# A two-layer graph kernel on one core: outgoing table cleared from ScalarE's queue, two chunks' degrees on VectorE, the last weight turned in node tiles 4 to 8

## The chip, the cores and the metric

The kernel runs on one core of a Trainium2 chip. The metric is the time of one execution on the device in microseconds. TensorE is PE, VectorE DVE, ScalarE ACT, GpSimd POOL and SyncE SP in the rows. SP computes nothing here: it issues loads and stores, one after the other, each behind its waits.

## What is computed

```python
def sage(h, W_self, W_neigh, b):            # deg_inv = 1 / max(in-degree, 1)
    agg = segment_sum(h[src], dst)
    return h @ W_self + (agg * deg_inv[:, None]) @ W_neigh + b

h   = relu(sage(x, W_self0, W_neigh0, b0))
x   = layernorm(x + sage(h, W_self1, W_neigh1, b1))
# GCN layer on x, with self loops, deg = out-degree + 1
y   = x @ W.T + b
msg = deg[row]**-0.5 * deg[col]**-0.5 * y[col]
out = layernorm(x + segment_sum(msg, row))
```

x is 1250 x 1024 in fp32, there are 20000 edges sorted by dst, and all five weights are 1024 x 1024.

## The kernel before

**Data.** The 1250 nodes are 10 tiles of 128 rows (the last has 98), the 1024 features 8 blocks (KD = 8). The graph becomes two dense tables of 1280 x 1280 counts in DRAM, `adj_in` and `adj_out`, 6.55 MB each. They are set to zero, then GpSimd scatters into them, 160 indirect DMAs of 125 numbers for each table. A table is read back in panels of 1280 x 256 (1280 KB). Every fp32 product is split: an operand is kept as a rounded high part (written by ScalarE) and the rest as low part (written by VectorE), and three matmuls stand for one.

**Stages on PE.** All have one order, written out by hand in program text.

- *Node tiles 0 to 9* (`linear(N0, t)`, L1429): x W_neigh0. A tile is 24 steps of two 512-wide matmuls; after step 4 the next x tile is transposed (`turn_tile`, L1370). ScalarE runs per tile `turn_hi(t + 1)`, `evict_hi(N0, t)` and `store_turned(t + 1)`, and VectorE the low parts. In the last tile ScalarE also splits the rows of W_self0 (`split_hi(S0, k)`), rows 0 to 3 ahead of `evict_hi(N0, 9)`.
- *self_turned* (L1484): x W_self0, turned, in 24 steps of 24 matmuls, chunks of 4, 4 and 2 node tiles. At the last step of a chunk its eight blocks are finished one by one; ScalarE evicts each into one of four `staged` slots and stores it to `s0t_scr` (`store_s0`). Block i waits for the store of block i - 4, and PE waits for the evicted bank before it opens the same bank in the next chunk.
- *mean0*: the neighbour sum, in four chunks of 2, 4, 2, 2 node tiles (`CHUNKS`), eight feature blocks each, so 32 cells m = 0 to 31, a cell being 20 matmuls (L1515) against the chunk's panels. At the head of a chunk PE makes the degrees: ten matmuls of ones against the panels (L1504). VectorE turns them into 1/deg (L1183, L1185), and then per cell scales the bank (L1191, frees it: `h_free`) and adds the self block that SP fetched from `s0t_scr` (L914, `h_sum`). After blocks 1 and 2 of a chunk it reduces panels for the out-degree (`dpart`, L1197). After block 2 PE turns 1/deg to columns by tiny matmuls (L1522), which VectorE copies to `dinv` after block 5.
- *products* (L1572): the two products of layer 1 by a seven-product scheme; *mean1* (L1589): neighbour sum and first layernorm, node tile by node tile, where after each of tiles 1 to 8 PE transposes one row block of the GCN weight (`turn_weights`, L1380), ScalarE copies it out (L857) and stores it to `wt_scr`; *gather* (L1606) and the last linear (L1429, L1413).

**SP in mean0.** The self fetches are issued in order of m. Four slots serve cells 0 to 15, so fetch m waits for `h_sum` m - 3 (from m = 4 on). Behind fetch 15 stand the panels of chunk 2, behind fetch 23 those of chunk 3; both also wait for their part of the scatters (`load_chunk_1`):

```python
            for m, (c, d) in enumerate(H_BLOCKS):                     # L509
                if m >= 4:
                    sp.wait_ge(h_sum, fetch_free(m))                  # m - 3 for m < 16
                sp.dma_start(fetch_slot(m)..., s0t_scr[...])          # L514
                if m in (15, 23):
                    load_chunk_1(2 + m // 17)                         # L425
```

**The outgoing table.** GpSimd clears `adj_out` with four DMAs in the middle of its first group of scatters (L636), writes the ones of its diagonal at group 5 (L655), and scatters into it after `adj_in`. The zeros lie where node tile 6 will be evicted, so `evict_hi(N0, 6)` waits for both clears.

## Time and profile before

| | us |
|---|---|
| median of 3 runs | 851.29 |
| lowest, highest | 848.52, 852.38 |
| the profiled execution, its own time | 849.59 |
| its span | 847.9 |

The profile has a page (busy time of each engine, the span in 40 slices, DMA queues, the chain of work that ended last, the costliest groups) and views that the trace answers: timelines of one engine, waits, and DMA issues in a window. A timeline row gives the start, the length, the line, the tile written and the ones read, and in brackets how long the engine stood idle before it and what released it. PE's rows are modelled, and a row reaches a little into the next, so the distance between starts is the better length.

### The profile page before, as it was taken

The page shows a single profiled execution, that of the slowest core. Times are in us where ns is not written, and L with a number is a line of the kernel's source. Part 1 is how long each engine was busy: PE and PEld are TensorE (multiplying, and loading weights), DVE is VectorE, ACT ScalarE, POOL GpSimd, SP SyncE. Part 2 cuts the span into 40 slices and gives each one's busy share as a digit, 9 for nine tenths or more (in the row PEclk, how much of TensorE's full clock was granted, in tenths as well). Part 3 has the DMA queues.
Part 4 walks back from the last instruction along what each step waited for, and adds up shares of the span by engine and source line. Part 5 has one row for each costly group of instructions (what it writes and reads, how often), then busy time and mean ns, then how long its engine had stood idle before and what let it go on. Part 6 is the DMA issues. An engine that isn't in the chain of part 4 may idle for free.

```text
span 847.9 us, 11000 instructions
## 1 busy us (share of the span) xinstructions
PE 830.6 (98%) x4295; PEld 707.9 (83%) x4295; DVE 461.3 (54%) x714; ACT 177.4 (21%) x218; POOL 459.1 (54%) x343
## 2 busy tenths in 40 slices
PE   8999999999999999999999999999999999999996
PEld 6888888888897899788888888778889889988885
DVE  6465568200017565897544677775556435455555
ACT  4111132110111113353123112222222122200000
POOL 5028887787777887885888788788620000000000
PEclk9999999999999999999999999999999999999999
DMA  9977965463776425668876668267877649555551
GB/s 332 380 304 267 350 193 168 125 176 75 213 236 180 122 57 133 249 237 286 298 282 222 243 220 284 62 176 214 240 245 255 223 150 295 189 199 199 198 193 46
DMA packets 99480, 180.52 MB, mean 213 GB/s; under 512 B 15474, under 2 KB 75898, under 8 KB 94048
## 3 DMA queue, kind: packets, MB, share of 16 engines
q1 hardware_dynamic: 60144, 124.17, 44.0%
q10 hardware_dynamic: 26896, 40.65, 13.3%
q0 software_dynamic: 12384, 14.95, 7.6%
q8 instruction: 36, 0.59, 0.3%
q14 instruction: 20, 0.16, 0.1%
HBM read 107.08 MB, written 72.43 MB: 212 GB/s over the span
## 4 chain that ended last, share of the span: by engine, by line
PE 61%; POOL 15%; DMA 9%; issue 8%; DVE 5%; SPq 1%; ACT 1%; POOLq 0%; ACTq 0%; DVEq 0%
PE ps L1572 19%; POOL adj_in L643 14%; PE ps L1429 12%; PE ps L1606 10%; PE ps L1589 9%; PE ps L1515 8%; DMA adj_in<-u 4%; DMA first_rows<-in_L_gnn_W_neigh 1%; DMA spare<-in_x 1%; DMA xin<-s0t_scr 1%; PE ps L1413 1%; DVE u L914 1%; PE ps L1380 1%; SPq L514 1%; DVE sacc L1303 0%
## 5 line engine op out<-in xcount | busy, mean ns | idle before, releaser
L643 POOL DMA_INDIRECT adj_out<-loops,idx_out x160 | 245.2, 1533 | 65.4 <-issue 65.4
L643 POOL DMA_INDIRECT adj_in<-mult,idx_in x160 | 198.1, 1238 | 86.8 <-issue 86.8
L1572 PE MATMUL ps<-u 128*128 128x512 f32 x840 | 190.7, 389 | 1.4 <-DVE u L914 1.4
L1572 PEld LDWEIGHTS ps<-u 128*128 128x128 f32 x840 | 157.6, 188 | 34.2 <-issue 1.6
L1484 PE MATMUL ps<-wx 128*128 128x512 f32 (+1 forms) x576 | 109.4, 351 | 1.3 <-ACT outb L761 1.3
L1484 PEld LDWEIGHTS ps<-wx 128*128 128x128 f32 x576 | 93.9, 189 | 16.9 <-ACT outb L761 1.9
L1429 PE MATMUL ps<-u 128*128 128x512 f32 x432 | 98.2, 389 | 0.0
L1515 PE MATMUL ps<-wx,u 128*128 128x256 f32 (+5 forms) x640 | 94.8, 309 | 1.2 <-DVE ht L1191 1.2
L1589 PE MATMUL ps<-u,panel_tiles 128*128 128x512 f32 (+1 forms) x400 | 93.9, 393 | 1.9 <-DVE u L914 1.9
L1429 PEld LDWEIGHTS ps<-u 128*128 128x128 f32 x432 | 81.0, 188 | 16.8
L1515 PEld LDWEIGHTS ps<-wx,u 128*128 128x128 f32 (+1 forms) x640 | 86.6, 191 | 8.2 <-DVE ht L1191 1.6
L1429 PE MATMUL ps<-wx 128*128 128x512 f32 x384 | 89.6, 392 | 0.0
L1589 PEld LDWEIGHTS ps<-u,panel_tiles 128*128 128x128 f32 (+1 forms) x400 | 74.5, 188 | 18.1 <-issue 2.3
L1429 PEld LDWEIGHTS ps<-wx 128*128 128x128 f32 x384 | 71.4, 188 | 14.6
L1606 PE MATMUL ps<-u,wx 128*128 128x512 f32 (+2 forms) x480 | 74.5, 317 | 0.0
L1606 PEld LDWEIGHTS ps<-u,wx 128*128 128x128 f32 x480 | 67.2, 191 | 6.6
L1183 DVE TENSOR_SCALAR dinv_row<-ps 128x256 f32<-128x256 f32 (+2 forms) x4 | 1.9, 480 | 84.7 <-PE ps L1504 84.7
L844 ACT ACTIVATE std<-mv,eps 128x1 f32<-128x1 f32 x20 | 5.9, 295 | 163.8 <-DVE mv L1028 163.8
L761 ACT ACTIVATE outb<-ps,b0c 128x512 f32<-128x512 f32 (+1 forms) x24 | 14.8, 618 | 94.1 <-PE ps L1484 87.2
L1347 DVE SCALAR_TENSOR_TENSOR outb<-ps,dscale,xin 128x1024 f32<-128x1024 f32 x9 | 11.6, 1283 | 40.8 <-PE ps L1429 40.8
L816 ACT ACTIVATE ht<-ht 128x256 f32<-128x256 f32 (+2 forms) x32 | 14.9, 466 | 83.1 <-DVE ht L914 83.1
L1006 DVE TENSOR_TENSOR u<-ps,u 128x1024 fp32r<-128x1024 f32 x10 | 12.2, 1224 | 33.3 <-ACT u L721 33.2
(167 smaller groups left out, 779.8 us busy)
## 6 DMA issues: line engine op xcount, KB each, us to landing
left_scr<-u SPq DMA_DIRECT2D x7, 2560.0 KB, 9.5
u<-left_scr SPq DMA_DIRECT2D x7, 2560.0 KB, 9.6
xt_scr<-wx ACTq DMA_DIRECT2D x10, 1024.0 KB, 9.9
u<-xt_scr SPq DMA_DIRECT2D x10, 1024.0 KB, 5.1
wx<-xt_scr SPq DMA_DIRECT2D x16, 512.0 KB, 4.0
adj_in<-u POOLq DMA_DIRECT2D x4, 1600.0 KB, 25.3
adj_out<-u POOLq DMA_DIRECT2D x4, 1600.0 KB, 16.1
wx<-adj_in SPq DMA_DIRECT2D x5, 1280.0 KB, 7.1
```

The source lines that it names most:

```text
L514: sp.dma_start(fetch_slot(m)[:, 0:CHUNKS[c][1] * T], s0t_scr[d, :, lines(CHUNKS[c])]).then_inc(s0_in[m % 8], 16)
L643: pool.indirect_dma_start(table, bass.IndirectOffsetOnAxis(ap=index[0:EP, j:j + 1], axis=0), counts[0:EP, j:j + 1], None, bounds_check=CEL ...
L761: nc.scalar.activation(staged[i % 4][:, 0:width], ps[:, d, 0:width], ACT.Identity, bias=b0c[:, d:d + 1]).then_inc(s0_free, 1)
L816: nc.scalar.activation(cell, cell, ACT.Relu).then_inc(h_done, 1)
L1006: nc.vector.tensor_tensor(u[:, :, t, 1, :], pair_bank(acc_pair(q, t)).rearrange("p (a j) -> p a j", a=2), u[:, :, t, 0, :].bitcast(F32), A ...
L1347: nc.vector.scalar_tensor_tensor(z, pair_bank(acc_pair(GCN, t))[:, :], dscale[:, t:t + 1], rest, ALU.mult, ALU.add).then_inc(acc_free, 1)
L1429: ins = nc.tensor.matmul(acc[:, cols], left_tile[:, t % 2, k, left * T:(left + 1) * T], w_row(q, k, right)[:, cols], start=(i == 0), stop= ...
L1484: ins = nc.tensor.matmul(block_of[d], w[:, k, left, d * P:(d + 1) * P], where[right], start=(first and left + right == 0), stop=(final and ...
L1515: ins = nc.tensor.matmul(ps[:, h_bank(m), 0:width].rearrange("p (n j) -> p n j", n=n // 2), typed(u0_part(k, h, d), exact), typed(panels[0 ...
L1572: ins = nc.tensor.matmul(ps[:, product_bank(g, i, p), :], left_op[n % 2][:, p, k, left, :], right_op[n % 2][:, k, right, :], start=(not on ...
L1589: ins = nc.tensor.matmul(pair_bank(acc_pair("MEAN1", t))[:, cols], typed(p1_tile[t][0:rows(k), k, :], exact), typed(u[0:rows(k), n, k, h, ...
L1606: ins = nc.tensor.matmul(ps[:, g_bank(KD * c + d), 0:width].rearrange("p (n j) -> p n j", n=n // 2), typed(yd[:, h, d * P:(d + 1) * P], ex ...
```

## The change

Five things are moved.

1. `adj_out` is cleared by five DMAs from ScalarE's queue in self_turned, after steps 2 to 6, from zeros that VectorE writes into `xin`. The diagonal follows from ScalarE before s0 block 8. GpSimd's clears and diagonal go, as does the wait of `evict_hi` for `cleared_out`. Since `xin` is the source, SP waits for the clears before it fetches self blocks, and it now fetches 0 to 3 at step 20 of self_turned.
2. The degrees of chunks 0 and 1: VectorE sums the panels over their ten row tiles (L1213 in the new file) into `sacc`, rounds them into `colsum`, and PE does one matmul of ones against it (`degrees`), after block 3 of the chunk.
3. The degrees of chunks 2 and 3 stay ten matmuls. The tiny turns of 1/deg go in all chunks: SP stores each row to `dinv_scr` and loads all as columns after mean0.
4. The turns of the GCN weight go from mean1 to node tiles 4 to 8, by `WEIGHT_ROWS`: row blocks 0; 1, 2; 3, 4; 5, 6; 7. They stand after steps 10 and 18 of the tile. SP loads them into `raw`, and the loads of the first rows of W_self0, which use `raw` and `outb`, wait for them.
5. `bias` and `colsum` share memory, so the load of b1 goes behind the degrees.

```diff
+    WEIGHT_ROWS = {4: (0,), 5: (1, 2), 6: (3, 4), 7: (5, 6), 8: (7,)}
...
             for t in range(2, NT):
                 load_x(t)
+                for k in WEIGHT_ROWS.get(t - 1, ()):
+                    sp.wait_ge(w_lo_done, KD * S0)
+                    if k >= 2:
+                        sp.wait_ge(wt_turned, k - 1)
+                    sp.dma_start(raw[:, k % 2, :], w_gcn[k * P:(k + 1) * P, :]).then_inc(wt_in[k % 2], 16)
             for k in range(4):
-                sp.wait_ge(w_lo_done, KD * S0)
+                if k < 2:
+                    sp.wait_ge(wt_turned, 7 + k)
+                else:
+                    sp.wait_ge(wt_stored[k % 2], 16 * KD // 2)
                 load_w(S0, k)
...
+                if i == 20:
+                    sp.wait_ge(adj_out_set, 16 * CLEARS)
+                    for m in range(4):
+                        fetch_self(m)
...
                 if m in (15, 23):
                     load_chunk_1(2 + m // 17)
+                if d == 6:
+                    t0, n = CHUNKS[c]
+                    sp.wait_ge(dinv_row_done, c + 1)
+                    sp.dma_start(dinv_scr[lines(CHUNKS[c])].rearrange("(a j) -> a j", a=1), dinv_row[0:1, c % 2, 0:n * T]
+                                 ).then_inc(dinv_stored[c % 2], 16)
...
+            def keep_turned(k):
+                act.wait_ge(wt_turned, k + 1)
+                if k >= 2:
+                    act.wait_ge(wt_stored[k % 2], 16 * (k // 2))
+                else:
+                    act.wait_ge(w_lo_done, KD * S0)
+                nc.scalar.activation(outb[:, k % 2, :], pair_bank(3), ACT.Copy).then_inc(wt_copied, 1)
...
                     turn_hi(t + 1)
+                    for k in WEIGHT_ROWS.get(t, ()):
+                        keep_turned(k)
                     evict_hi(N0, t)
...
+            for a in range(CLEARS):
+                act.wait_ge(*s0_used_by(a + 2))
+                act.dma_start(runs[a, :, :, :], zeros_out.unsqueeze(1).broadcast_to([P, ZERO_TIMES, ZERO_PART])).then_inc(adj_out_set, 16)
...
                 if d == 0:
+                    if c < 2:
+                        dve.wait_ge(m1_full[c], 16 * n // 2)
+                        nc.vector.tensor_reduce(sacc[:, 0:width].rearrange("p (n j) -> p n j", n=n // 2),
+                                                m1_panels[c][:, :, :, :].bitcast(F32).rearrange("p k n j -> p n j k"), AX_X, ALU.add
+                                                ).then_inc(colsum_done, 1)
+                        dve.wait_ge(colsum_done, 2 * c + 1)
+                        nc.vector.tensor_copy(colsum[:, 0:width], sacc[:, 0:width]).then_inc(colsum_done, 1)
                     dve.wait_ge(deg_full, c + 1)
...
-                        if d == 2:
-                            pe.wait_ge(dinv_row_done, c + 1)
-                            for i in range(n):
-                                ins = nc.tensor.matmul(ps[:, 6 + c % 2, i:i + 1], dinv_row[0:1, c % 2, i * T:(i + 1) * T],
-                                                       ones_nt[0:1, 0:1], start=True, stop=True)
-                            ins.then_inc(dcol_full, 1)
+                        if (c, d) in ((0, 3), (1, 3)):
+                            degrees(c, width, exact)
```

The order of instructions at three places. First PE in mean0, chunks 0 to 2. `ones_r` is the operand of ones; the rows of before:

```order
L1504 MATMUL ps<-wx,ones_r 128x256 x10
L1515 MATMUL ps<-wx,u 128x256 x60
L1522 MATMUL ps<-ones_nt,dinv_row 128x1 x2
L1515 MATMUL ps<-wx,u 128x256 x100
L1504 MATMUL ps<-wx,ones_r 128x512 x10
L1515 MATMUL ps<-wx,u 128x512 x60
L1522 MATMUL ps<-ones_nt,dinv_row 128x1 x4
L1515 MATMUL ps<-wx,u 128x512 x100
L1504 MATMUL ps<-wx,ones_r 128x256 x10
```

and of the change:

```order
L1563 MATMUL ps<-wx,u 128x256 x80
L1540 MATMUL ps<-colsum,ones_r 128x256
L1563 MATMUL ps<-wx,u 128x256 x80
L1563 MATMUL ps<-wx,u 128x512 x80
L1540 MATMUL ps<-colsum,ones_r 128x512
L1563 MATMUL ps<-wx,u 128x512 x80
L1551 MATMUL ps<-wx,ones_r 128x256 x10
```

The degrees of chunk 1 stood ahead of its first cell and now stand behind its fourth (80 matmuls are four cells).

Second VectorE, from the last cell of chunk 0 to the first two of chunk 1, before:

```order
L1191 TENSOR_TENSOR ht<-ps,dinv_row 128x256
L914 SCALAR_TENSOR_TENSOR ht<-ht,xin 128x256
L1183 TENSOR_SCALAR dinv_row<-ps 128x512
L1185 RECIPROCAL dinv_row<-dinv_row 128x512
L1191 TENSOR_TENSOR ht<-ps,dinv_row 128x512
```

and in the change:

```order
L1229 TENSOR_TENSOR ht<-ps,dinv_row 128x256
L943 SCALAR_TENSOR_TENSOR ht<-ht,xin 128x256
L1213 TENSOR_REDUCE sacc<-wx 128x512
L1217 CAST colsum<-sacc 128x512
L1221 TENSOR_SCALAR dinv_row<-ps 128x512
L1223 RECIPROCAL dinv_row<-dinv_row 128x512
L1229 TENSOR_TENSOR ht<-ps,dinv_row 128x512
```

The reduction and the rounding stand ahead of the row work, which waits for the one matmul, and with it everything behind.

Third PE in node tile 5 of the change, between the turns of x tiles 6 and 7 (L1406; `raw` holds the weight rows); before, 48 matmuls stood there in one piece:

```order
L1406 MATMUL ps<-ident,xin 128x128 x8
L1468 MATMUL ps<-wx 128x512 x12
L1417 MATMUL ps<-ident,raw 128x128 x8
L1468 MATMUL ps<-wx 128x512 x16
L1417 MATMUL ps<-ident,raw 128x128 x8
L1468 MATMUL ps<-wx 128x512 x20
L1406 MATMUL ps<-ident,xin 128x128 x8
```

Two blocks of eight transposes came in; the eight blocks of this kind between the tiles of mean1 went out.

## Rows read from the trace of the kernel before

**Rows 1.** Page: busy us, share, instructions; then the granted TensorE clock by slice (9: 90% or more).

```profile
PE 830.6 (98%) x4295; PEld 707.9 (83%) x4295; DVE 461.3 (54%) x714; ACT 177.4 (21%) x218; POOL 459.1 (54%) x343
...
PEclk9999999999999999999999999999999999999999
```

**Rows 2.** Waits of PE: line, releaser, us in total, times, longest.

```profile
PE ps L1589 <- DVE u L914: 1.9, 1, 1.9
...
PE ps L1380 <- ACT late L857: 1.1, 1, 1.1
```

**Rows 3.** PE's timeline, mean0: start us, us, line, shapes, count, [idle before <-releaser].

```profile
237.41 1.37 PE L1504 MATMUL ps<-wx,ones_r 128*128 128x256 f32 x10
238.62 7.36 PE L1515 MATMUL ps<-wx,u 128*128 128x256 f32 x60
245.91 0.60 PE L1522 MATMUL ps<-ones_nt,dinv_row 1*128 1x1 f32 x4
246.44 12.26 PE L1515 MATMUL ps<-wx,u 128*128 128x256 f32 x100
258.54 2.46 PE L1504 MATMUL ps<-wx,ones_r 128*128 128x512 f32 x10
262.19 14.04 PE L1515 MATMUL ps<-wx,u 128*128 128x512 f32 x60 [1.20 <-DVE ht L1191]
276.16 1.05 PE L1522 MATMUL ps<-ones_nt,dinv_row 1*128 1x1 f32 x8
277.14 23.22 PE L1515 MATMUL ps<-wx,u 128*128 128x512 f32 x100
300.19 1.35 PE L1504 MATMUL ps<-wx,ones_r 128*128 128x256 f32 x10
```

**Rows 4.** VectorE's timeline, mean0: second self add, then chunk 1's row work, cells, reduction.

```profile
258.32 0.43 DVE L914 SCALAR_TENSOR_TENSOR ht<-ht,xin 128x256 f32<-128x256 f32 x1 [4.12 <-DMA xin<-s0t_scr]
...
267.10 0.68 DVE L1183 TENSOR_SCALAR dinv_row<-ps 128x512 f32<-128x512 f32 x1
...
271.21 0.69 DVE L1191 TENSOR_TENSOR ht<-ps,dinv_row 128x512 f32<-128x512 f32 x1
...
273.87 2.81 DVE L1197 TENSOR_REDUCE dpart<-wx 128x10 f32<-128x2560 f32 x1
```

**Rows 5.** SP's queue, mean0: issue of fetches 5 to 15, then of chunk 2's panels.

```profile
258.83 25.08 SPq L514 DMA_DIRECT2D xin<-s0t_scr  x11
287.54 0.37 SPq L425 DMA_DIRECT2D wx<-adj_in  x1
```

**Rows 6.** DMA issues (at 224, 240 and 69 us; then of the whole run): KB each, median us to landing.

```profile
wx<-adj_in SPq DMA_DIRECT2D x1, 1280.0 KB, 6.4
...
wx<-adj_in SPq DMA_DIRECT2D x1, 1280.0 KB, 12.8
...
xt_scr<-wx ACTq DMA_DIRECT2D x1, 1024.0 KB, 4.2
...
wt_scr<-late ACTq DMA_DIRECT2D x8, 512.0 KB, 5.0
...
raw<-in_L_gnn_W_self SPq DMA_DIRECT2D x4, 512.0 KB, 10.5
```

**Rows 7.** PE's timeline: a turn block in node tile 8, one in mean1.

```profile
105.99 1.04 PE L1370 MATMUL ps<-ident,xin 128*128 128x128 f32 x8
106.79 1.40 PE L1429 MATMUL ps<-wx 128*128 128x512 f32 x5
...
575.06 1.04 PE L1380 MATMUL ps<-ident,late 128*128 128x128 f32 x8
```

**Rows 8.** ScalarE's timeline, self_turned: evictions 0 and 4 of the s0 blocks.

```profile
165.87 0.69 ACT L761 ACTIVATE outb<-ps,b0c 128x512 f32<-128x512 f32 x1 [32.51 <-PE ps L1484]
...
170.30 0.69 ACT L761 ACTIVATE outb<-ps,b0c 128x512 f32<-128x512 f32 x1 [0.46 <-PE ps L1484]
```

**Rows 9.** PE's timeline, start of the kernel.

```profile
1.47 4.21 PE L1634 MATMUL ps<-ones_r 128*128 128x512 f32 x9 [1.47 <-DVE scrap_dve L1043]
```

137 lines of the change are left out of this document (71 added, 66 removed).

## The prediction, made before the changed kernel ran

> **What bounds the kernel now.** The page's engine row comes first: PE is busy 830.6 us of a span of 847.9 us and its granted clock reads 9 in every slice [rows 1]. So PE never rests: 17.3 us of idle is all that removed waits can give, the rest must come out of PE's own list. The list of PE's waits says which part of that idle this change can reach: 1.1 us at L1380, released by ScalarE's copy of a turned weight [rows 2], and 1.20 us in mean0 at L1515, released by VectorE [rows 3]. The chain of waits is less use: a third of it is GpSimd's scatters and the loads behind them, but PE was working through nearly all of that time. So I read PE's own timeline through mean0 [rows 3], then the engines that feed PE there.
>
> **1. Degrees of chunks 0 and 1, and the turning of 1/deg.** PE drops ten 256-wide column sums (237.41 to 238.62, 1.21 us) and ten 512-wide ones (ten at 4.61/20 = 0.23 us, 2.30 us, from the cell duration below) and gets one matmul of each width, 0.12 and 0.23 us. It also drops the small turns L1522: 245.91 to 246.44 is 0.53 us for two node tiles (records 245.91 x4), 276.16 to 277.14 is 0.98 us for four, and chunks 2 and 3 have two node tiles each. Sum: (1.21 - 0.12) + (2.30 - 0.23) + 3 x 0.53 + 0.98 = 1.09 + 2.07 + 2.57 = 5.73 us off PE [rows 3]. The 1.20 us wait of 262.19 goes too: VectorE was late there since its second self block landed only at 258.3 [rows 4], behind the panels of chunk 1 on SP's queue. The change fetches blocks 0 to 3 in self_turned. Together 6.93 us.
>
> What VectorE gets: a reduction of 2560 numbers, then one of 5120. The nearest row is the contiguous reduction of 2560, 2.81 us [rows 4]; the new ones read with a stride, which no row shows. I take 2.8 and 5.5 us, and twice that as the bad bound. The first lies in front of mean0, where VectorE has nothing to do. The second starts after cell 7, about 24 us into mean0, and must be done at 38 us, when PE has finished cell 11: covered by 8 us, and by 2.5 us at the bad bound.
>
> **2. What is late next: chunk 2's panels.** This is the part that decides. The degree matmul of chunk 1 now stands behind cell 11 (four cells into the chunk) and not ahead of cell 8. VectorE can't scale any cell of the chunk before it, so four cells pile up. From the start of the chunk's row work (267.10) to the first cell's scaling (271.21) is 4.11 us; two cells take 273.87 - 271.21 = 2.66 us, so 1.33 each; a dpart reduction takes 2.81 us and its short sum about 0.2 more [rows 4]. To the end of cell 11: 4.11 + 4 x 1.33 + 2 x 3.0 = 15.4 us, 15.6 with the last write. And SP's queue has h_sum 12 in it: fetch_self(15) waits for cell 11, since slot 15 mod 4 is the slot of 11, and the panels of chunk 2 are issued behind it (m in (15, 23)). Before, SP issued fetch 15 as the last of eleven, ending at 283.91, then stood until GpSimd's 144th scatter had landed and issued the panels at 287.54, still 12.6 us before PE wanted them at 300.19 [rows 3, 5].
>
> Count from mean0's start. Chunk 0: eight cells of 12.10/5 = 2.42 us (246.44 to 258.54) and one short matmul, 19.5 us. Cells 8 to 11: 4 x 4.61 (23.05/5, from 277.14 to 300.19) = 18.5 us, so the degree matmul goes at 38.0 and ends at about 38.4. Cell 11 is added at 38.4 + 15.6 = 54.0. SP issues fetch 15 and then the panels, at 54.5. A load of that size from this table took 6.4 us to landing when alone, 12.8 us behind its twin [rows 6]; with the small fetch 15 ahead I take 6.8, so 61.3. PE is through cell 15 at 19.5 + 36.9 + 0.23 = 56.7. It waits 61.3 - 56.7 = **4.6 us**, where it waited for nothing; the landing alone spreads this from 4.2 to 10.6. Net of mean0: -6.93 + 4.6 = -2.3 us. Nothing else there is late: cell 14 wants cell 8's bank back, free at 38.4 + 4.8 = 43.2 against 47.4; chunk 1's panels are issued earlier against PE than before, because GpSimd's list is shorter and PE comes later; stored 1/deg rows come back on SP long before mean1.
>
> **3. The weight turns.** Eight blocks of eight transposes leave mean1 and enter node tiles 4 to 8. A block is 1.04 us long in a node tile and in mean1, and the matmuls after it start 0.8 us behind its start [rows 7], so 6.4 us are moved and none saved; what goes is the 1.1 us wait at L1380 [rows 2]. ScalarE's eight copies, 1.4 us each at most by the 0.69 us of half the width [rows 8], go to an engine that is 21% busy [rows 1] and are waited for only by the next block, 16 matmuls later. Loads: each of rows 2 to 7 is issued when the row two before it is turned, a node tile (48 matmuls of 0.23 us, 11 us) or more ahead of use; a 512 KB load must stay under that. The tightest link is at the end: the store of row 7, then self weight row 3 into the same outb slot, then ScalarE's evict_hi(9), in order behind that split. The turn of x tile 9 stands at 105.99 [rows 7], and seven blocks by then shift it to 111.6; 0.8 us and twelve matmuls of 0.23 later row 7 is turned, done by 116.0; copied by 117.0; a store of a turned row took 5.0 us and a load of such a weight row 10.5 in traffic [rows 6], and no more than the store's 5 on a quiet queue, so row 3 lands between 127 and 132.5. PE leaves tile 9 at 111.6 + 0.8 + (28 + 12 + 48 matmuls) x 0.23 + 0.8 = 133.4, and only then has ScalarE anything to evict. Covered by 1 to 6 us, and PE wants that bank 18 matmuls later still. Cost taken: 0, bounds 0 and 3.
>
> **4. The outgoing table.** GpSimd loses four clears and two diagonal stores from its queue and is done with its scatters a little earlier. Nothing of it shows in PE's time: chunk 2's panels now wait for VectorE, and chunk 3's had landed in time before, with PE now later. The clears go to ScalarE's queue, the fifth at the end of self_turned's step 6, about 1 us before the stores of the finished s0 blocks. Those stores share its queue, and the eviction of block 4 waits for store 0. Before, eviction 0 started at 165.87 and eviction 4 at 170.30, so each took 1.11 us and the eighth was done at about 174.4 [rows 8]. PE had finished block 0 at 165.6 and wanted the eighth bank 42 matmuls later (21 of the rest of step 7, 21 of step 8), at 175.2: 0.8 us to spare. The fifth clear is issued at 164.9 in those times. A 1024 KB store landed in 4.2 us [rows 6], so 1280 KB take 5 to 7 us beside the loads of that stage, store 0 lands at 171 to 173, and eviction 4 starts 0.6 to 2.7 us late. Cost 0 to 1.9 us; I take **0.5**.
>
> The row shows no store queued behind a clear. The Trainium skill (DMA: Bandwidth & Descriptors, section "Queues, rings and completion order") says that one issuing engine's DMAs use the same rings and are consumed in ring order; by that the store waits for the clear as I assumed. If DMAs of one queue overtook each other, this cost would be 0.
>
> **Sum.** -6.93 + 4.6 - 1.1 + 0.5 = -2.9 us. Against the profiled execution of 849.6 us (span 847.9) that is 846.7 us, -0.34%; the median of the runs shown is 851.29 us, 1.7 us higher, so 848.4 us.
>
> **The rivals.**
> A. *Chunk 2's panels are not late.* If SP didn't have to wait for cell 11, or VectorE caught up faster, the 4.6 us fall away: 848.4 - 4.6 = 843.8 us. For it: the wait depends on a slot number and on rows that I had to move. Against: every link is in program order, and the 15.6 us are measured. A shorter stall of 2 to 3 us, which is in reach of my errors, gives 846 to 847.
> B. *PE's clock falls in the new gap.* All slices of before stand at 2.4 GHz [rows 1], and the longest idle among them is 1.9 us [rows 2]. At the start of the kernel nine matmuls took 4.21 us, 0.47 each against 0.23 [rows 9], so PE ran for that stretch at half rate. If a 4.6 us gap brings that back, the same stretch costs 4.21 - 9 x 0.23 = 2.1 us more: 848.4 + 2.1 = 850.5 us, no change. The Trainium skill (TensorE: Matmul & The Clock Gate, section "HAM oscillation") says that a PE that waits for a transfer long enough is put back to half rate and starts slow again; this is that rule's time here, and no gap of before is long enough to show it.
> C. *The panel transfer lands late.* It costs 12.8 us, as for the twin at 240, and not 6.8: PE waits 10.6 us, the sum is +3.1, and with the clock fallen (+2.1) it is +5.2 us: 856.5 us, slower. It decides above 9.7 us of landing. For it: the same table's load did take that long when two were issued together. Against: here one is issued alone, and SP's next transfers stand behind it.
>
> **Numbers.** The forecast with its errors (846.5 to 850) gets 0.52; A 0.20; B 0.15; C and a late weight row in part 3 0.13. A measurement of this kernel can tell about 0.5%, or 4.3 us, from no change; the forecast of -2.9 us lies within that, but near its edge, so a share of it counts as faster. Faster by over 0.5%: 0.20 from A and 0.12 from the forecast's edge, 0.32. Slower by over 0.5%: 0.10. Within: 0.58. The range reaches from A, 843.5, to past B, 852.5.
>
> **What would show it.** PE's timeline in mean0: about 19.5 us for chunk 0, then a gap of 4.6 us ahead of the ten column sums of chunk 2, released by a DMA into wx from adj_in; no gap ahead of cell 8. SP's timeline: the panels of chunk 2 issued 54 us after mean0's start. VectorE: a reduction of about 5.5 us behind cell 7. ScalarE: the eviction of s0 block 4 starts 1 to 3 us later than its cadence. PE's waits: L1380's is gone, no new one in node tiles 4 to 8, nor at self_turned's first blocks. The granted clock: full in the slice after the gap; below it for B. I am wrong if the gap is absent, if it is longer than 6 us, or if a wait for a weight row shows up in the first 130 us.

## The result, and the profile after

The changed kernel takes 852.25 us (median of 16 runs, 850.04 to 857.51), the kernel before in the same session 849.93 us (16 runs, 847.78 to 852.38): ratio 1.0032, 95% interval 1.0021 to 1.0043. So it is slower by 0.3%, where 848.4 us was forecast, that is 2.9 us off the 851.29 us of the three runs of before known then; off the 849.93 us measured beside the changed kernel it would have been 847.0. The profiled execution took 850.04 us (span 848.3). It is the fastest of the 16, and its mean granted clock is 0.996, while most of the others lie between 0.989 and 0.994.

Of both kernels the execution with the trace is compared below; for the kernel before that is a typical one (849.59 us), for the changed kernel its fastest.

The page's engine row, as [rows 1]: PE has 3.3 us less to do, and the span is 0.4 us longer.

```profile
PE 827.3 (98%) x4257; PEld 703.5 (83%) x4257; DVE 476.0 (56%) x715; ACT 178.6 (21%) x218; POOL 456.7 (54%) x337
```

PE's waits, as [rows 2]. L1380's wait is gone. New are the wait at L1551 (the column sums of chunk 2), 1.87 us of the 3.0 at L1523 (self_turned; the rest stood in before too) and a small one at the gather (L1648).

```profile
PE ps L1551 <- DMA wx<-adj_in: 5.0, 1, 5.0
PE ps L1523 <- ACT outb L797: 3.0, 6, 1.0
PE ps L1616 <- DVE u L943: 1.6, 1, 1.6
...
PE ps L1648 <- DMA panel_tiles<-adj_out: 0.5, 1, 0.5
```

PE's timeline through mean0, as [rows 3] (L1563 the cells, L1540 the one matmul of degrees, L1551 the ten of chunks 2 and 3):

```profile
247.74 9.76 PE L1563 MATMUL ps<-wx,u 128*128 128x256 f32 x80
257.33 0.28 PE L1540 MATMUL ps<-colsum,ones_r 128*128 128x256 f32 x1
257.45 28.12 PE L1563 MATMUL ps<-wx,u 128*128 128x256 f32 x160
285.41 0.39 PE L1540 MATMUL ps<-colsum,ones_r 128*128 128x512 f32 x1
285.64 18.53 PE L1563 MATMUL ps<-wx,u 128*128 128x512 f32 x80
309.12 2.49 PE L1551 MATMUL ps<-wx,ones_r 128*128 128x256 f32 x10 [4.95 <-DMA wx<-adj_in]
311.40 19.88 PE L1563 MATMUL ps<-wx,u 128*128 128x256 f32 x160
331.12 1.28 PE L1551 MATMUL ps<-wx,ones_r 128*128 128x226 f32 x10
```

No gap stands ahead of cell 8. The gap ahead of chunk 2 is there. Behind it the ten sums take 311.40 - 309.12 = 2.28 us, where ten such sums took 1.21 us before [rows 3]. The granted clock by windows tells why (columns: window, its length with the busy us of PE, PEld, DVE, ACT, POOL, then PEclk, DMA share, GB/s):

```profile
305.00:309.00 4.00, 0.00 (x0) 0.00 (x0) 3.95 (x4) 0.63 (x1) 3.41 (x2) 1.00 1.08 335
309.00:313.00 4.00, 3.88 (x19) 3.88 (x20) 1.32 (x2) 0.63 (x1) 3.38 (x3) 0.57 0.63 143
313.00:317.00 4.00, 4.00 (x36) 4.00 (x35) 1.79 (x4) 0.42 (x1) 3.09 (x4) 1.00 0.17 34
```

SP's queue, as [rows 5], and VectorE's second reduction, as [rows 4]:

```profile
266.49 30.99 SPq L476 DMA_DIRECT2D xin<-s0t_scr  x8
...
302.05 0.37 SPq L432 DMA_DIRECT2D wx<-adj_in  x1
...
319.55 0.37 SPq L432 DMA_DIRECT2D wx<-adj_in  x1
```

```profile
270.65 9.46 DVE L1213 TENSOR_REDUCE sacc<-wx 128x512 f32<-128x5120 f32 x1
280.14 0.43 DVE L1217 CAST colsum<-sacc 128x512 fp32r<-128x512 f32 x1
```

The reduction took 9.46 us, the first one 4.80 (from 241.58), where I had 5.5 and 2.8 and twice that as the bad bound. It ended 4.8 us before the matmul at 285.41.

In self_turned PE waits four times for ScalarE's evictions when it opens the banks again, 1.87 us together. The three matmuls behind each of the first three waits take 0.96 us, 0.32 each and not 0.23, so the stage loses more than the waits say:

```profile
181.26 0.96 PE L1523 MATMUL ps<-wx 128*128 128x512 f32 x3 [0.96 <-ACT outb L797]
182.76 0.96 PE L1523 MATMUL ps<-wx 128*128 128x512 f32 x3 [0.54 <-ACT outb L797]
183.91 0.96 PE L1523 MATMUL ps<-wx 128*128 128x512 f32 x3 [0.18 <-ACT outb L797]
185.05 2.33 PE L1523 MATMUL ps<-wx 128*128 128x512 f32 x9 [0.19 <-ACT outb L797]
```

The chain of waits (start, length, what) has changed its last part. In the changed kernel it runs through GpSimd up to the gather:

```profile
626.50 2.57 DMA adj_out<-loops,idx_out
629.09 6.54 DMA panel_tiles<-adj_out
635.68 13.48 PE ps L1648 x110
```

GpSimd's last scatter starts at 626.50 us. Before it started at 620.33. That bears on every mending below, and [rows 1 to 9] don't have it:

```profile
620.33 1.27 POOL L643 DMA_INDIRECT adj_out<-loops,idx_out  x1 [0.30 <-issue]
```

Set side by side, the starts of PE's stages say where the time went (us; the shift is the changed kernel's start less before's):

| PE starts | before | changed | shift | shift that the prediction's terms give |
|---|---|---|---|---|
| self_turned | 126.86 | 133.90 | 7.0 | 6.4 |
| mean0 | 237.41 | 247.74 | 10.3 | 6.9 |
| products | 342.64 | 351.82 | 9.2 | 4.6 |
| mean1 | 535.24 | 543.06 | 7.8 | 4.6 |
| gather | 635.34 | 635.68 | 0.3 | -2.9 |

The biggest step that wasn't forecast is self_turned. It takes 113.8 us and took 110.6, so 3.3 us more, where the term was 0.5. On the page its matmuls, 576 in both kernels, are busy 1.4 us longer and waited 1.7 us longer for ScalarE:

```profile
L1484 PE MATMUL ps<-wx 128*128 128x512 f32 (+1 forms) x576 | 109.4, 351 | 1.3 <-ACT outb L761 1.3
L1523 PE MATMUL ps<-wx 128*128 128x512 f32 (+1 forms) x576 | 110.8, 352 | 3.2 <-ACT outb L797 3.0
```

The rows of the later stages, before and changed:

```profile
342.64 190.66 PE L1572 MATMUL ps<-u 128*128 128x512 f32 x840 [1.43 <-DVE u L914]
535.24 18.57 PE L1589 MATMUL ps<-u,panel_tiles 128*128 128x512 f32 x80 [1.94 <-DVE u L914]
351.82 190.68 PE L1616 MATMUL ps<-u 128*128 128x512 f32 x840 [1.56 <-DVE u L943]
543.06 92.10 PE L1633 MATMUL ps<-u,panel_tiles 128*128 128x512 f32 x400 [0.56 <-DVE u L943]
```

### The profile page after: what moved, and what is told of

Read it like the earlier page. It is cut to its first block, busy times and chain, and to the rows that moved or that the text cites. A ratio compares the mean times of both kernels' runs of the same rounds, so it can differ in the third digit from the quotient of the medians.

```text
span 848.3 us, 10948 instructions
## 1 busy us (share of the span) xinstructions
PE 827.3 (98%) x4257; PEld 703.5 (83%) x4257; DVE 476.0 (56%) x715; ACT 178.6 (21%) x218; POOL 456.7 (54%) x337
## 2 busy tenths in 40 slices
DMA packets 102815, 180.52 MB, mean 213 GB/s; under 512 B 18038, under 2 KB 78465, under 8 KB 97896
## 4 chain that ended last, share of the span: by engine, by line
POOL 47%; PE 23%; issue 19%; DMA 7%; DVE 1%; POOLq 1%; SPq 0%; ACT 0%; DVEq 0%
POOL adj_out L663 26%; POOL adj_in L663 21%; PE ps L1468 12%; PE ps L1648 10%; DMA adj_in<-u 4%; DMA first_rows<-in_L_gnn_W_neigh 1%; PE ps L1450 1%; POOLq L663 1%; DMA panel_tiles<-adj_out 1%; DVE sacc L1339 0%; SPq L426 0%; DMA adj_out<-loops,idx_out 0%; PE ps L1669 0%; POOL adj_in L660 0%; DVE outb L1355 0%
## 5 line engine op out<-in xcount | busy, mean ns | idle before, releaser
L1523 PE MATMUL ps<-wx 128*128 128x512 f32 (+1 forms) x576 | 110.8, 352 | 3.2 <-ACT outb L797 3.0
L1523 PEld LDWEIGHTS ps<-wx 128*128 128x128 f32 x576 | 93.7, 189 | 20.4 <-ACT outb L797 5.4
L1563 PE MATMUL ps<-wx,u 128*128 128x256 f32 (+5 forms) x640 | 94.3, 309 | 0.0
L1633 PE MATMUL ps<-u,panel_tiles 128*128 128x512 f32 (+1 forms) x400 | 92.1, 392 | 0.6 <-DVE u L943 0.6
L1563 PEld LDWEIGHTS ps<-wx,u 128*128 128x128 f32 (+1 forms) x640 | 87.1, 192 | 6.6
L1468 PE MATMUL ps<-wx 128*128 128x512 f32 x384 | 91.9, 394 | 0.0
L1648 PE MATMUL ps<-u,wx 128*128 128x512 f32 (+2 forms) x480 | 74.5, 317 | 0.0
L1648 PEld LDWEIGHTS ps<-u,wx 128*128 128x128 f32 x480 | 67.2, 191 | 6.6
L1213 DVE TENSOR_REDUCE sacc<-wx 128x256 f32<-128x2560 f32 (+1 forms) x2 | 14.3, 7129 | 79.3 <-DMA wx<-adj_in 79.3
```

The lines of the kernel that those rows point to most:

```text
L1213: nc.vector.tensor_reduce(sacc[:, 0:width].rearrange("p (n j) -> p n j", n=n // 2), m1_panels[c][:, :, :, :].bitcast(F32).rearrange("p k n ...
L1468: ins = nc.tensor.matmul(acc[:, cols], left_tile[:, t % 2, k, left * T:(left + 1) * T], w_row(q, k, right)[:, cols], start=(i == 0), stop= ...
L1523: ins = nc.tensor.matmul(block_of[d], w[:, k, left, d * P:(d + 1) * P], where[right], start=(first and left + right == 0), stop=(final and ...
L1563: ins = nc.tensor.matmul(ps[:, h_bank(m), 0:width].rearrange("p (n j) -> p n j", n=n // 2), typed(u0_part(k, h, d), exact), typed(panels[0 ...
L1633: ins = nc.tensor.matmul(pair_bank(acc_pair("MEAN1", t))[:, cols], typed(p1_tile[t][0:rows(k), k, :], exact), typed(u[0:rows(k), n, k, h, ...
L1648: ins = nc.tensor.matmul(ps[:, g_bank(KD * c + d), 0:width].rearrange("p (n j) -> p n j", n=n // 2), typed(yd[:, h, d * P:(d + 1) * P], ex ...
```

## The theories

- **W, the waits.** The change loses its savings in the three new waits: chunk 2's panels, the evictions, and the clock behind them. Mended one by one, they give 3 to 7 us back.
- **H, GpSimd.** GpSimd's scatters bind as closely as PE's list did. Whatever PE saves ahead of a table is waited off when it wants the table. (For the gather alone the expectations call it G; other letters in them are explained where they stand.)
- **K, the clock.** A gap in PE's work costs more than its length, since the clock is lower behind it.

Three sessions of runs (e1 to e4, e9 to e12, e13 to e16) were made on chips where the kernel before takes 849.8 to 850.3 us. One, with e5 to e8, was made on a chip where it takes 871.0 us. So ratios to the kernel before of the same session are compared.

## Experiments on single parts

**e1, chunk 2's panels early.** Changed kernel with

```diff
-                if m in (15, 23):
+                if m in (13, 23):
                     load_chunk_1(2 + m // 17)
```

> The change, with chunk 2's panels issued behind self fetch 13 and not behind fetch 15, so that SP no longer waits for cell 11 before it issues them. Theory G (GpSimd's last scatter into the outgoing table, 6 us later than before the change, holds the start of the gather, so what PE saves ahead of it is lost): the 5.0 us wait and the slow start behind it go from mean0, a wait of 4 to 7 us appears ahead of the gather's first matmul, released by the load of the outgoing panels, and the time stays within 1.5 us of the change's 852.3. Theory P (PE's list and its own waits add up to the time, as I predicted): 5.0 us of wait and 1.4 us of half rate go, 846 us.

Measured: 852.44 us, ratio 1.0022 [1.0000, 1.0044]. The gap ahead of chunk 2 is gone, and the time is not. PE's waits:

```profile
PE ps L1648 <- DMA panel_tiles<-adj_out: 4.9, 1, 4.9
PE ps L1523 <- ACT outb L797: 2.1, 3, 1.1
PE ps L1616 <- DVE u L943: 1.9, 1, 1.9
PE ps L1551 <- DMA wx<-adj_in: 1.4, 1, 1.4
```

The wait of 5 us moved 330 us down the program, to the gather, released by the load behind GpSimd's last scatter. Another 1.4 us stands at chunk 3's column sums, and the granted clock is at 0.50 from 634 to 640 us, behind the wait at the gather.

**e2, e3, e4, the last 16 scatters into adj_out left out**, in the changed kernel, in e1 and in before:

```diff
-                for j in range(EC):
+                for j in range(EC - 16):
                     put(adj_out, idx_out, loops, j, scattered_out)
...
-            sp.wait_ge(scattered_out, 16 * EC)
+            sp.wait_ge(scattered_out, 16 * (EC - 16))
```

> The change, with the last 16 of the 160 scatters into the outgoing table left out, so GpSimd is done some 24 us earlier (those edges are missing from the second layer's sum). Theory G: the wait ahead of the gather, 0.5 us in the profiled execution and more in the typical one, goes; 849.5 to 851.5 us. Theory P: no change beyond 0.5 us, 851.8 to 852.5 us. Rival T (the clock after the 5 us gap varies between executions): no change either, with the same spread.

> The change, with chunk 2's panels behind fetch 13 and with the last 16 scatters into the outgoing table left out (those edges are missing from the second layer's sum). Theory G: only both together give the whole, 5.0 + 1.4 us of mean0 and the wait ahead of the gather: 843 to 846 us, at least 5 us under each of the two alone. Theory P: the same as the panels alone, 846 us.

> The kernel before, with the last 16 scatters into the outgoing table left out (those edges are missing from the second layer's sum). Theories G and P both: before the change the last scatter had landed 1 us before SP was free to load the panels, so nothing moves, ratio 0.999 to 1.001. If the ratio is under 0.998, the outgoing table held the kernel before too in its typical execution.

Measured: e2 855.71 us, ratio 1.0064 [1.0043, 1.0086]; e3 848.35, 0.9989 [0.9968, 1.0011], above the 843 to 846 us that I expected; e4 849.56, 0.9991 [0.9975, 1.0006]. No gather wait is left in e2 and e3. Against e1, e3 gives back 4.1 us, about what the gather had waited. Before gains nothing: its gather isn't held by GpSimd. e2 is a miss. It has six runs, and a mean clock of 0.992 like the changed kernel's. Its waits are the changed kernel's without the gather, with 3.1 us ahead of the products and not 1.6. Why it is 3 us slower is not explained. Its trace shows something else. Up to the last 16 scatters e2 is the changed kernel, and yet its 160th scatter starts at 307.27 us, where the changed kernel's starts at 316.49 and before's at 309.77. So when GpSimd comes to a table differs by 9 us between two executions of the same instructions, and e2 is slow with an early GpSimd: GpSimd can't be the whole cause of the changed kernel's time.

**e5, the turns back in mean1.** Changed kernel without part 3:

```diff
-                    if q == N0 and i in (10, 18) and i // 18 < len(WEIGHT_ROWS.get(t, ())):
-                        turn_weights(WEIGHT_ROWS[t][i // 18])
...
+                        if 1 <= t <= KD:
+                            turn_weights(t - 1)
```

(and the loads, copies and stores with them).

> The change without its third part: the weight is turned in mean1 again, its loads and stores with it; degrees and the clears from ScalarE's queue stay. Theory G (every wait of PE costs its length and, when it is 2 us or more, a stretch at half rate; the last scatter holds the gather since the rows' traffic in node tiles 4 to 8 slows GpSimd there): no wait ahead of the gather, last scatter at 617 to 621 us and not 626.5; the waits at the evictions (1.9 us) and for chunk 2's panels (5.0 and 1.4 us of half rate) stay; 850.5 to 852.5 us. Theory W (the turns in the node tiles themselves cost the time): 849 us or less. If GpSimd's last scatter stays at 626, the clears are what slows it.

**e6, the clears back on GpSimd.** Changed kernel without part 4:

```diff
-                act.wait_ge(*s0_used_by(a + 2))
-                act.dma_start(runs[a, :, :, :], zeros_out.unsqueeze(1).broadcast_to([P, ZERO_TIMES, ZERO_PART])).then_inc(adj_out_set, 16)
...
+                        if (g, c) == (0, RUN // 2) and not general_form:
+                            clear(adj_out, cleared_out)
```

> The change without its fourth part: GpSimd clears the outgoing table and writes its diagonal again; degrees and early turns stay. Theory G: no wait at the evictions of self_turned beyond the 1.3 us of before, full rate there; GpSimd's list is 4 us longer, so its last scatter starts at 628 to 631 us and the wait ahead of the gather grows from 0.5 to 4 to 7 us; 850 to 853 us. Theory P (waits add up, no GpSimd bound): 849 us.

**e7, part 1 alone**, the degrees in the kernel before (with the early self fetches):

```diff
+                    if c < 2:
+                        dve.wait_ge(m1_full[c], 16 * n // 2)
+                        nc.vector.tensor_reduce(sacc[:, 0:width]...)
...
+                        if (c, d) in ((0, 3), (1, 3)):
+                            degrees(c, width, exact)
```

> The change's first part alone (degrees of two chunks on VectorE, 1/deg by way of memory): turns in mean1 and clears on GpSimd as before. By my sum: 6.9 us off, 5.0 us of wait for chunk 2's panels and 1.4 us of half rate behind it on, so 849.3 us, ratio 0.998 to 1.001. It measures whether this part is worth anything as it stands.

**e8, three things mended**: e5 with e1's edit and the clears a step earlier:

```diff
             for a in range(CLEARS):
-                act.wait_ge(*s0_used_by(a + 2))
+                act.wait_ge(*s0_used_by(a + 1))
```

> Turns in mean1 as before, degrees as changed with chunk 2's panels issued behind self fetch 13, clears from ScalarE's queue one step earlier each (after steps 1 to 5). Theory G: no wait at chunk 2, the evictions' waits back at 1.3 us, GpSimd early, so the full 6.9 us of mean0: 842 to 845 us, ratio 0.991 to 0.994. Theory P gives the same here. If the evictions still wait, the five clears disturb them by their load and not by the place of the last one.

Measured on the chip where before takes 871.03 us:

| | us | ratio | 95% |
|---|---|---|---|
| e5, turns back | 874.82 | 1.0050 | 1.0026 to 1.0073 |
| e6, clears back | 883.12 | 1.0160 | 1.0135 to 1.0185 |
| e7, part 1 alone | 869.70 | 0.9993 | 0.9972 to 1.0013 |
| e8, three mended | 863.52 | 0.9923 | 0.9901 to 0.9945 |

Part 1 alone takes 5.7 us of work off PE and gains nothing that can be measured: its panels of chunk 2 come 4.7 us late too. In e6 PE waits 10.6 us in the node tiles for a copy of a turned weight row, which stands on ScalarE behind `evict_hi(N0, 6)` and its wait for GpSimd's clears. So part 4 is what makes part 3 possible. Three expectations were missed here: e5's last scatter starts at 626.13 us and not at 617 to 621, e6 doesn't wait at the gather, and e6 is far above its 850 to 853 us even as a ratio. By e5's own words the clears would then be what slows GpSimd, but e8 has them on ScalarE's queue too, and its last scatter starts at 617.64. e8 looked like the answer, 0.8% faster than before.

## The same edits on a chip like the first

**e9**: changed kernel with e1's and e8's edits, turns in the node tiles. **e10**: with the clears' edit alone. **e11**: e5 with e1's edit. **e12**: e8 once more.

> The change with two edits: chunk 2's panels issued behind self fetch 13 (before fetches 14 and 15), and each of the five clears of adj_out one step earlier in self_turned. The turns of the weight stay in node tiles 4 to 8; that alone sets it apart from the kernel with three edits, which measured 0.9923 of before. Theory G (with the panels early, GpSimd's last scatter holds the gather, and the moved turns are what PE no longer has in mean1 to cover it): a wait at the gather, released by the DMA panel_tiles<-adj_out, of 4 to 6 us, no wait of over 1 us at the column sums, the eviction waits in self_turned under 1 us; ratio to before 0.995 to 1.000, so some 3 to 5 us above the kernel with the turns in mean1. Rival (where the turns stand makes no difference, and the kernel with three edits is fast because of the clears alone): no wait or a small one at the gather, ratio 0.990 to 0.994.

> The change with one edit: each of the five clears one step earlier in self_turned, so that the fifth is issued a whole step (24 matmuls) before the first s0 store and not about 1 us before it. If the fifth clear holds store 0 and so eviction 4, the four waits that summed to 1.87 us around 181 to 185 fall to under 0.4 us, the slice 180 to 200 us stays at the full granted clock, and the ratio is 0.996 to 1.001 (the change: 1.0032). The waits at chunk 2's column sums (about 5 us) and at the gather (about 0.5, up to 3 since PE comes earlier) stay. Rival (the evictions are late from a DMA load of that stage, whatever stands before them on ScalarE's queue): the same waits, ratio 1.002 to 1.004.

> The change with the turns of the weight in mean1 as before and chunk 2's panels behind self fetch 13; the clears stay where the change has them. It differs from the kernel with three edits (0.9923 of before) by the step of the clears alone. If the clears' place is worth the eviction waits and a stretch at the lower clock, 2 to 4 us: ratio 0.995 to 0.998, waits at self_turned's evictions 2 to 4 us. If the clears' place is worth little and the panels and the turns made it: 0.991 to 0.993. No wait at chunk 2's column sums over 1.5 us and none at the gather.

> The kernel with three edits once more (turns in mean1 as before, panels behind fetch 13, clears a step earlier), on this chip and beside the other three. It measured 0.9923 [0.9901, 0.9945] on a chip where both kernels were 2.5% slower. If it is worth its 6 to 7 us wherever it runs: 0.990 to 0.995. If that was the other chip, on which PE's clock fell more often: 0.996 to 0.999, which is what the sum of its parts gives from the profile alone (5.73 + 1.2 of part 1, less some of the new waits).

Measured (before 850.27 us, 27 runs):

| | turns | panels | clears | us | ratio | 95% |
|---|---|---|---|---|---|---|
| e9 | node tiles | early | early | 849.60 | 1.0005 | 0.9983 to 1.0026 |
| e10 | node tiles | as changed | early | 851.90 | 1.0021 | 1.0001 to 1.0041 |
| e11 | mean1 | early | as changed | 852.82 | 1.0037 | 1.0025 to 1.0049 |
| e12 | mean1 | early | early | 853.44 | 1.0047 | 1.0028 to 1.0066 |

e12 is e8, and it is slower than before here. e9, e11 and e12 came out above every ratio that I had written down for them or for the theory behind them, e9 without the wait at the gather that I expected (0.4 us), and e10 in the rival's range although its waits fell as in the first theory. W is not enough, then, and the trace of the mended kernel had to say more. PE's timeline and SP's queue of e12 in mean0 (L1554 the column sums of chunks 2 and 3):

```profile
298.62 2.26 PE L1554 MATMUL ps<-wx,ones_r 128*128 128x256 f32 x10 [1.87 <-DMA wx<-adj_in]
324.31 2.48 PE L1554 MATMUL ps<-wx,ones_r 128*128 128x226 f32 x10 [3.54 <-DMA wx<-adj_in]
```

```profile
317.88 0.37 SPq L432 DMA_DIRECT2D wx<-adj_in  x1
```

and GpSimd's last scatter into adj_in, the 160th:

```profile
314.50 1.19 POOL L664 DMA_INDIRECT adj_in<-mult,idx_in  x1 [0.30 <-issue]
```

PE waits for chunk 3's panels, which SP issues when that scatter has landed. The load lands 6.4 us later, at 324.3, and neither SP's queue nor VectorE has a part in it. The same three rows of the kernel before read: scatter 160 at 309.77, panels issued at 314.12 and 7.1 us to landing, so 321.2; and PE begins these sums at 321.30 without idle time:

```profile
309.77 1.19 POOL L643 DMA_INDIRECT adj_in<-mult,idx_in  x1 [0.30 <-issue]
```

```profile
314.12 0.37 SPq L425 DMA_DIRECT2D wx<-adj_in  x1
```

```profile
wx<-adj_in SPq DMA_DIRECT2D x1, 1280.0 KB, 7.1
```

```profile
321.30 1.32 PE L1504 MATMUL ps<-wx,ones_r 128*128 128x226 f32 x10
```

So before had 0.1 us to spare at this place, and its list of waits shows nothing there. With GpSimd as it ran in that execution and PE's order otherwise unchanged, no microsecond saved ahead of chunk 3 could have been kept. Behind both waits of e12 the clock is at half as well (0.50 from 300 to 302 and from 324 to 328 us).

On the slower chip PE needs longer up to chunk 3 and GpSimd doesn't: scatter 160 starts at 314.28 us in e8 and at 314.50 in e12, and PE makes the degrees of chunk 1 at 286.91 and at 277.99. PE reached chunk 3's sums at 326.17 us in e8, 2.9 us after its panels were due (issued 316.92, plus 6.4), and waited for nothing. That fits a gain there and a loss here. It isn't shown, since no run on the slower chip shortens GpSimd's list and before has no trace there.

## GpSimd's list shortened, and one gap by itself

**e13, e14, e15**: in e12, e9 and before the last 8 of 160 scatters into adj_in are left out, so that all that GpSimd does behind them comes about 12 us earlier (8 times 1.5).

```diff
-                        put(adj_in, idx_in, mult, g * RUN + c, scattered_in[sum(g >= need for need in NEEDS)])
+                        if (g, c) < (GROUPS - 1, RUN - 8):
+                            put(adj_in, idx_in, mult, g * RUN + c, scattered_in[sum(g >= need for need in NEEDS)])
```

(and SP's wait for the last part of the scatters lower by 8.)

> The kernel with three edits (turns in mean1 as before, panels behind fetch 13, clears a step earlier; 1.0047 of before) with the last 8 of 160 scatters into adj_in left out, so that its table lacks 1000 of 20000 edges; everything on GpSimd behind them, the whole of adj_out too, comes 12 us earlier (8 times 1.5). Theory H (GpSimd's scatters and the load behind them set the start of chunk 3 at 321 to 325 us whatever PE does, and later the gather, so that what PE saves before is waited off): the 3.5 us wait at chunk 3's column sums goes, the gather waits for nothing, and the ratio falls from 1.0047 to 0.994 to 0.999. Rival (the savings are lost to the lower clock and to ScalarE's and VectorE's waits, and the wait at chunk 3 would come out elsewhere): ratio 1.001 to 1.005.

> The kernel with two edits (turns in node tiles 4 to 8, panels behind fetch 13, clears a step earlier; 1.0005 of before) with the last 8 of 160 scatters into adj_in left out. Theory H: here the turns stand ahead of mean0 and fill the time that would be waited off, so chunk 3 hardly waited, but the gather is near its bound; PE's list is then the bound in both kernels and this one comes out near the one with the turns in mean1: 0.993 to 0.998, a gain of 0.3 to 0.6%. Rival: no gain, 0.999 to 1.002.

> Control: the kernel before with the last 8 of 160 scatters into adj_in left out. Its chunk 3 started exactly when its panels had landed (321.2 against 321.30) and without idle time, so PE's list was just the bound and nothing is gained: 0.998 to 1.001 by either theory. A ratio under 0.997 would say that before waited for GpSimd in many of its executions, though not in the profiled one.

**e16**, one gap in the kernel before:

```diff
-                if m in (15, 23):
-                    load_chunk_1(2 + m // 17)
+                if m in (20, 23):
+                    load_chunk_1(2 + m // 23)
```

> The kernel before with one edit: chunk 2's panels are issued behind self fetch 20 and not 15. Fetch 20 waits for cell 14, which is added at about 298 us, so the panels land at about 304.5 and PE waits some 4 us ahead of chunk 2's column sums, which stand at 300.19. Nothing else changes. If a wait costs its own length alone: +4 us, ratio 1.004 to 1.006. If the clock falls behind it as in the changed kernel (ten sums in 2.28 us and not 1.21) and PE goes slower for that stretch only: +5 to +6 us, 1.006 to 1.008. If chunk 3's start is pinned by its panels at 321 us plus, and the gap pushes everything: the same, since chunk 3's panels then have landed in time.

Measured (before 849.94 us, 17 runs):

| | us | ratio | 95% | same kernel with all scatters |
|---|---|---|---|---|
| e13, turns in mean1 | 846.53 | 0.9953 | 0.9938 to 0.9968 | 1.0047 (e12) |
| e14, turns in node tiles | 841.48 | 0.9898 | 0.9885 to 0.9911 | 1.0005 (e9) |
| e15, before | 849.31 | 0.9997 | 0.9984 to 1.0010 | 1 |
| e16, one gap | 857.73 | 1.0096 | 1.0081 to 1.0111 | |

With 8 scatters fewer both mended kernels gain 0.9 to 1.1% and before gains nothing. The control matters: if 8 scatters fewer were worth time by themselves, e15 would show it. For the kernel with the turns in mean1, H is shown. The last scatter into adj_in starts at 302.99 us in e13 and at 314.50 in e12, 11.5 us earlier; the 3.54 us wait at chunk 3 is gone, and mean0 takes 103.7 us where it took 107.8, which is most of the 4.6 us between the two spans. For e9 and e14 the medians agree with H and the traces show little of it, as told below. e14 waits for no panels at all; its longest waits are:

```profile
PE ps L1498 <- ACT wx L724: 1.6, 1, 1.6
PE ps L1524 <- DMA wx<-xt_scr: 1.6, 1, 1.6
PE ps L1617 <- DVE u L944: 1.6, 1, 1.6
```

e14 came out better than I expected (0.993 to 0.998), and better than e13 by 5 us, as e9 is better than e12 by 4. e13 still waits 3.8 us at chunk 2, whose panels stand behind scatter 144, and that one isn't moved by leaving out the last 8. With the turns in the node tiles PE comes to mean0 about 8 us later (degrees of chunk 0 at 257.03 us in e14, 249.45 in e13), so GpSimd is further on: work put ahead of a table is time that GpSimd gets. The traces of e13 and e14 differ in a second thing that isn't in the edit. At its 40th scatter GpSimd stood still for 7.34 us in e13 and for 2.39 in e14, and scatter 144 starts at 290.63 and at 283.50. So the 5 us between them are not the turns' place alone. Nor do the traces settle e9 against e14: e9's profiled execution (845.8 us, the fastest of its twelve) has no wait at chunk 3 and 0.4 us at the gather, its span is only 2.7 us longer than e14's, and 1.5 of these stand in self_turned, ahead of the scatters left out. The other 5 us of the medians lie in executions without a trace, whose mean clocks go down to 0.989.

K is shown by e16. The gap is one wait of 3.94 us, ahead of the sums that stood at 300.19 before, and the granted clock is at half (1.2 of 2.4 GHz) for some 6 us behind it:

```profile
304.29 2.51 PE L1504 MATMUL ps<-wx,ones_r 128*128 128x256 f32 x10 [3.94 <-DMA wx<-adj_in]
```

```profile
304.00:306.00 2.00, 1.72 (x8) 1.72 (x9) 0.00 (x0) 0.00 (x0) 1.70 (x2) 0.50 0.51 107
306.00:308.00 2.00, 2.00 (x11) 2.00 (x11) 1.14 (x2) 0.00 (x0) 1.65 (x2) 0.50 0.06 1
308.00:310.00 2.00, 2.00 (x12) 2.00 (x11) 1.04 (x1) 0.00 (x0) 1.43 (x2) 0.54 0.06 1
```

From chunk 2's sums to chunk 3's PE takes 327.95 - 304.29 = 23.66 us, where before took 321.30 - 300.19 = 21.11, so the wait cost its length and 2.6 us more. Against before's trace the gather starts 641.36 - 635.34 = 6.0 us later, and the two profiled executions are 6.1 us apart. The medians say 7.8 us, above my highest expectation of 6. A short wait can do it too: in e1 the clock is at 0.50 from 184 to 186 us, behind waits of 1.09 and 0.41 us for evictions, while the changed kernel's four waits at the same place left it at 1.00. So no length above which the clock falls can be read from these runs, and the 2 us of e5's expectation isn't borne out.

Each run comes with its mean granted clock. Mean time times mean clock of a kernel's runs is about the time that it would have at the full clock, and splits a kernel's time in two:

| | mean us | mean clock | product |
|---|---|---|---|
| before (17 runs, session of e13 to e16) | 849.8 | 0.9969 | 847.1 |
| changed kernel | 852.4 | 0.9928 | 846.2 |
| e9, two mended | 850.3 | 0.9933 | 844.7 |
| e12, three mended | 853.8 | 0.9920 | 847.0 |
| e13 | 846.6 | 0.9947 | 842.1 |
| e14 | 841.8 | 0.9974 | 839.7 |
| e16 | 857.7 | 0.9918 | 850.6 |

This is an estimate. By it, at the full clock the changed kernel would be 0.9 us faster than before. It is 2.6 us slower in the mean since it loses 0.41% more of its time to the clock, 3.5 us (its own session's before, whose clocks aren't on record, has a mean of 850.1 us, so 2.3 us). e16 splits into 3.5 us of gap and 4.4 us of clock. In e14, where PE waits for no table, the clock is back.

## Why the prediction was wrong, step by step

The change was forecast to be 2.9 us faster and is slower, 0.4 us by the profiled executions and 2.3 by the medians; the 1.9 us between the two go with the lower mean clock of most executions (0.993 in the mean, 0.996 in the profiled one). The time lies inside the stated range, but that is no merit of the sum. By the two traces the 3.2 us between the sum and PE's start of the gather are these terms: self_turned 2.8 us more than the 0.5 taken for the evictions, mean0 1.2 us more (1.07 of it the clock behind the gap, rival B, which isn't in the sum), the gather's wait 0.5 (GpSimd, taken as nothing), the turn blocks 0.1 (0.6 more in the node tiles and 0.5 more saved in mean1), and 1.4 us back at the head of mean1, where a wait of 1.94 us became 0.56 and no term stood. So two steps of the prediction failed, both in part 4 ("I take 0.5" for the evictions, and "Nothing of it shows in PE's time" for GpSimd), and rival B stood beside the sum and belonged in it. The parts one by one:

**Part 1 was right in its work.** The degree matmul of chunk 1 came 285.41 - 247.74 = 37.7 us after mean0's start (38.0 predicted), and the 1.20 us wait of [rows 3] went. Its size is shown where chunk 2's panels aren't late and nothing else waits long: mean0 takes 105.2 us before and 97.9 in e3 and e9, 7.3 us less, where the sum was 6.93.

**Part 2 was right.** SP issued the panels 302.05 - 247.74 = 54.3 us after the start (54.5), they landed 7.0 us later (6.8), and PE waited 4.95 us (4.6). The cause is confirmed by e1: two fetches earlier, and the gap is gone.

**Rival B is missing from the sum.** The sums behind the gap took 1.07 us more in the profiled execution, and the lower mean clocks of most other executions say that the kernel loses more there. I gave B 0.15 on the ground that no gap of before was long enough to show it [rows 1, 2]. e16 has a gap of 3.94 us and the fall with it. The Trainium skill (TensorE: Matmul & The Clock Gate, section "HAM oscillation") says that a PE that waits long enough for a transfer is put back to half rate; both traces agree, with 0.57 in the changed kernel's window at 309 to 313 and 0.50 in e16's.

**Part 3 was too low a gain.** No wait appeared in the node tiles and L1380's went. A tile with two blocks takes 13.6 us and one with one 12.7, so a block costs 0.9 us where I had 0.8. In the mended kernels the turns in the node tiles are worth more than the 1.1 us that I had: 3.8 us in the medians of e9 against e12 and 5.0 of e14 against e13, though part of the latter is GpSimd's shorter stop. I had looked at PE's list and not at what GpSimd does meanwhile.

**Part 4, the evictions: the term mis-sized most.** The waits come to 1.87 us, the bad bound, where I took 0.5, and eviction 4 started 180.52 - 172.91 = 7.6 us behind eviction 0 and not 4.4. The stage as a whole took 3.3 us more, beyond the bad bound, since the matmuls between the waits are longer too. With the clears a step earlier these waits are 0.19 us in e10 and none in e12, e13 and e14; without that edit they are 1.5 us in e1 and 2.7 in e11. So the fifth clear ahead of the stores is a cause, and not the only one, since e9 has the edit and one wait of 1.39 us. The length of self_turned says the same: 110.6 to 112.2 us in before, e4, e15 and e16, 113.8 to 115.5 in the changed kernel, e1, e2, e3 and e11, and 112.3 to 114.1 in e9, e10, e12, e13 and e14, which have the clears a step earlier. What else the clears from ScalarE's queue do to that stage stays open. The Trainium skill (DMA: Bandwidth & Descriptors, section "Queues, rings and completion order") says that on each ring descriptors are consumed in ring order, though DMAs need not complete in the order of issue. These runs fit the first half: in the changed kernel eviction 4 idles 2.67 us for a store issued behind the fifth clear, and 1.23 us in e10. What the edit is worth in time, 0.3 us between the medians of e10 (851.90) and the changed kernel (852.25, another session), is within the measurement.

**Part 4, GpSimd: the step that failed for every gain beyond the sum.** "GpSimd loses four clears and two diagonal stores from its queue and is done with its scatters a little earlier. Nothing of it shows in PE's time ... chunk 3's had landed in time before, with PE now later." GpSimd does show, by 0.5 us at the gather here and by 4.9 us in e1, where A's 843.8 us was to be had. Chunk 3's panels had landed in time before, but by 0.1 us, and the changed kernel didn't wait there only since it came 9.8 us later; e12 waits 3.54. And GpSimd, with 2.23 + 1.84 = 4.1 us less to issue, was later in the profiled execution, 6.7 us at scatter 160 and 6.2 us at the last one:

| start of scatter | 1 | 39 | 40 | 87 | 88 | 160 | 320 |
|---|---|---|---|---|---|---|---|
| before, us | 58.3 | 121.3 | 122.8 | 199.2 | 200.7 | 309.8 | 620.3 |
| changed | 59.3 | 118.0 | 126.0 | 202.1 | 207.2 | 316.5 | 626.5 |

It stands still again and again, from the 200th scatter on every 39 of them (200, 239, 278, 317) in both kernels. The first such stop follows the scatter of 135.99 before and takes 2.35 us; in the change it follows that of 118.03 and takes 6.60 us. In e2, the same program up to there, it takes 2.39:

```profile
118.03 1.36 POOL L663 DMA_INDIRECT adj_in<-mult,idx_in  x1 [0.30 <-issue]
125.99 2.03 POOL L663 DMA_INDIRECT adj_in<-mult,idx_in  x1 [6.60 <-issue]
```

```profile
119.52 1.19 POOL L663 DMA_INDIRECT adj_in<-mult,idx_in  x1 [2.39 <-issue]
```

```profile
135.99 1.19 POOL L643 DMA_INDIRECT adj_in<-mult,idx_in  x1 [0.30 <-issue]
139.53 1.19 POOL L643 DMA_INDIRECT adj_in<-mult,idx_in  x1 [2.35 <-issue]
```

The profile names no releaser. Full DMA engines don't explain the length: from 120 to 125 us their share is 0.86 in the changed kernel, 0.93 in e2 and 0.85 in e14, whose stop takes 2.39 us as well. e5 has a distance of 7.7 us between the two scatters, as the changed kernel has 8.0, without the loads of part 3. What makes the stops stays open, and so does which part of the 6.7 us is whose: from scatter 1 to scatter 160 e6, which has part 3 and no part 4, needs 256.7 us, e5 (part 4 and no part 3) 256.2, e7 (neither) 250.7, the changed kernel 257.2, before 251.5, and e2 249.2 with both parts in.

**Rivals A and C.** A's condition is e1, and A said 843.8 us. The gap at chunk 2 went, and a wait of 4.9 us came at the gather, at 852.44 us. With the gather's wait gone too (e3) it is 848.35 us, still above A. C didn't happen: the panels landed in 7.0 us.

So what was taken off and put on PE's list was predicted well, and what the moved work does around it wasn't: the clears to the evictions, the gap to the clock, and GpSimd's chain, which ran nearly as long as PE's and which a list of PE's waits doesn't show.
